# Preparing the next sequence inside the last head pair of a latent-attention stage: two tiles per step, projections spread over steps, score pieces inside the output tiles

## The chip, the cores and the metric

The kernel runs on one NeuronCore of one Trainium2 chip. The metric is the device time of one execution in microseconds (us). The kernel before takes 2420.44 us (median of 3 runs, 2420.27 to 2422.87).

## What is computed

A transformer-like stack on x of shape (2, 1024, 256) in float32: a mixture of experts, attention, the experts again, a LoRA mixture, a latent attention, and the LoRA mixture again. The change touches the latent attention alone. The reference of that part, for two sequences of 1024 tokens and 16 heads (8 pairs of heads):

```python
c_q = _rmsnorm(x @ Wq_down, q_norm_w)                       # 48 wide
q = (c_q @ Wq_up).reshape(b, s, H, HD).transpose(0, 2, 1, 3)
q_rope = _apply_rope((x @ Wq_rope).reshape(b, s, H, RD), cos, sin)
c_kv = _rmsnorm(x @ Wkv_down, kv_norm_w)                    # 64 wide
k = (c_kv @ Wk_up).reshape(b, s, H, HD).transpose(0, 2, 1, 3)
v = (c_kv @ Wv_up).reshape(b, s, H, HD).transpose(0, 2, 1, 3)
k_rope = _apply_rope((x @ Wk_rope).reshape(b, s, H, RD), cos, sin)
scores = (einsum(q, k) + einsum(q_rope, k_rope)) * (HD + RD) ** (-0.5)
out = einsum(softmax(scores), v)
out = out.transpose(0, 2, 1, 3).reshape(b, s, H * HD) @ Wout
```

x enters through a layer norm, and the result is added to x.

## The kernel before, in words

`mla_stage` (from L1475 on) writes one program for each engine by hand and orders them with semaphores; no scheduler stands between. Each sequence b has 8 head pairs. A pair (`pair`) is 16 steps s: the queries come in two blocks of 512 (s < 8 and s >= 8), and in each block the keys in 8 tiles of 128. In a step TensorE computes the scores of one key tile for both heads (`scores_of`, L1752, six matmuls of 512 columns, since each float32 product is made of three reduced ones), ScalarE takes the exponentials into PT (`exp_of`, L1930), TensorE multiplies the latent values with the probabilities of the step before (`values_of`, L1761), and GpSimd adds up the probabilities (`sums`, L1654). At the end of a block TensorE brings the sums across partitions (`denominators`, L1768), and VectorE inverts them (`reciprocals`, L2074, four instructions) and writes the block's latent output LA (`latent_out`, L2079).

Ahead of a pair stand its row maxima. They come from rough scores in pieces (`rough_scores`, L1733, one matmul of 512 columns each), each reduced by VectorE (`maxima`, L2062) into MXP. Of the 32 pieces of a pair, 22 (NLATE) are made before its step 0, in PSUM banks B and C in turn, and 10 in steps 2 to 6 (EARLY), all in bank A. `block_max` (L2068), `max_rows` (L1740, four transposes) and `max_copies` (L1917) turn the maxima into a row of the query operand.

Before its first pair a sequence needs a front: `normalized` (L160: the rows of 128 tokens, in one of two buffers), `xn_transposes` (L1673), `high_rows` (L1875) and `low_rows` (L2014), which split them into a high and a low part; `down_projection` (L1683, six matmuls of 112 columns a tile), `latents` (squares and a copy, L1882 and L1884); then for all tiles `latent_scales` (L2020 to L2028: mean squares, a reciprocal, and 16 instructions that write the normalised latents CN), with `latent_deviations` on ScalarE between them (a square root, with an activation table load before and after it); `latent_transposes` (L1690), `latent_highs` (L1893) and `latent_lows` (L2033); and the first pair's projections (`first_projections`, L1701 and L1708), their rotary products on VectorE (`first_rotary`, L2042 to L2049), the high parts on ScalarE (`highs`, L1905) and the low parts on VectorE (`lows`, L2056). SyncE places the parts in the operand buffers by DMA (`placed`, L1595 and L1599); half 1 of the projections may not be rotated before the DMAs of half 0 have landed, since they read the same buffers, and the next pair's rough scores wait for all of them.

For the second sequence this front is woven into the last pair (pair 7) of the first sequence, in the branches `if after`. Each engine has such branches, at the same steps: one tile of 128 tokens per step in steps 0 to 8, the scales in step 9 (RMS_AT), the latent transposes in steps 10 and 11 (TURN_AT), and half 0 and half 1 of the projections in steps 12 and 13 (FIRST_AT), each half in one go:

```python
RMS_AT, TURN_AT, FIRST_AT = TB + 1, (TB + 2, TB + 3), (TB + 4, TB + 5)
BESIDE = 3
```

After the last pair comes the output projection of the sequence, 8 tiles of `up_projection` (L1781, PSUM banks 4 and 5 in turn) with `updated` on VectorE (L2151, L2153), and beside it the 22 rough pieces of the next pair: two before the first tile, then BESIDE pieces behind each tile.

The functions that the diff touches, and what calls them:

## Time and profile before

| | |
|---|---|
| median of 3 runs | 2420.44 us |
| profiled execution, its own time | 2423.66 us |
| its span, first to last instruction | 2421.9 us |
| PE, DVE, ACT, POOL busy | 83%, 53%, 33%, 33% of the span |
| mean granted TensorE clock | 0.92 of full speed |
| first matmul of the first sequence's pair 7, step 0 | 1712.17 us |
| first matmul of its output projection | 1803.93 us |
| first matmul of the second sequence's pair 0 | 1847.62 us |

PE is TensorE, DVE VectorE, ACT ScalarE, POOL GpSimd, SPq the DMA queue of SyncE. Times in rows are us from the span's start. In a timeline row the first number is the start, the second the duration, and the bracket at the end the idle time of the engine just before and who ended it. The busy share is an average over the whole program; the change lies in the 135 us from 1712 to 1848, so the rows come from there.

### The profile page before, as it was taken

Reading aid. Unit: us, or ns where it says so; the run is one execution under the profiler, and the core shown is the slowest. Engines: PE = TensorE matmul, PEld = TensorE weight load, DVE = VectorE, ACT = ScalarE, POOL = GpSimd, SP = SyncE. Lnnn points to the kernel's source line nnn. Section 1 sums busy time; section 2 is a strip of 40 time slices with the busy share of each in tenths; the row PEclk is TensorE's granted clock in tenths of the full one; section 3 lists DMA queues with packets and bytes.
Section 4 is the critical chain, followed back from the end, with each engine's and each line's share of the span. In section 5 each row is a group of like instructions: output and inputs, shape, how many; then the busy total and the mean of one; then the engine's idle time right before and its main releaser. Section 6 shows DMA issues by size and latency. Waiting matters only on the chain. (4 is left out here: it accounts for less than half of the span.)

```text
span 2421.9 us, 30646 instructions
## 1 busy us (share of the span) xinstructions
PE 2018.4 (83%) x8676; PEld 1249.4 (52%) x8677; DVE 1283.6 (53%) x2888; ACT 790.0 (33%) x1298; POOL 805.5 (33%) x622
## 2 busy tenths in 40 slices
PE   4499947899898569982669999999969999999996
PEld 4266624555454446652545555555546555555465
DVE  3322245677775512224546666666655666666525
ACT  1022232554545112221223333333422333333312
POOL 2200051221212400005004555555522555555631
PEclk9999967899989579995758999999989999999998
DMA  7311133222320821124032222222031222222101
GB/s 311 137 61 61 61 99 38 35 27 28 52 27 1 345 77 60 59 67 149 6 78 48 53 53 52 52 52 52 5 78 30 50 50 52 52 52 52 29 1 46
DMA packets 85575, 159.78 MB, mean 66 GB/s; under 512 B 14881, under 2 KB 49265, under 8 KB 83185
## 3 DMA queue, kind: packets, MB, share of 16 engines
q1 hardware_dynamic: 63216, 127.25, 20.3%
q0 software_dynamic: 6144, 16.79, 2.1%
q10 hardware_dynamic: 16128, 14.69, 1.7%
q8 instruction: 42, 0.69, 0.1%
q14 instruction: 45, 0.36, 0.1%
HBM read 69.34 MB, written 27.39 MB: 40 GB/s over the span
## 5 line engine op out<-in xcount | busy, mean ns | idle before, releaser
L1654 POOL TENSOR_TENSOR mla_PS<-mla_PS,mla_PT 128x1024 f32<-128x1024 f32 x192 | 458.1, 2386 | 240.9 <-ACT mla_PT L1930 238.4
L2062 DVE TENSOR_REDUCE mla_MXP<-PS 128x1 f32<-128x512 f32 x512 | 342.3, 688 | 232.7 <-PE PS L1733 228.2
L1930 ACT ACTIVATE mla_PT<-PS 128x1024 f32<-128x1024 f32 x256 | 262.6, 1026 | 393.7 <-PE PS L1752 393.3
L1761 PE MATMUL PS<-mla_PT,mla_CN 128*64 128x512 f32 x1024 | 276.1, 618 | 0.2
L1733 PE MATMUL PS<-mla_KH,mla_QH 113*128 113x512 f32 x512 | 213.1, 454 | 35.4 <-DVE mla_MXP L2062 17.9
L446 DVE COPY moe_HT<-PS 128x512 f32<-128x512 f32 x96 | 66.4, 691 | 319.3 <-PE PS L556 313.1
L1752 PE MATMUL PS<-mla_QH,mla_KH 113*128 113x512 f32 x512 | 213.1, 416 | 0.3 <-ACT mla_QH L1917 0.3
L1752 PE MATMUL PS<-mla_QL,mla_KH 113*128 113x512 f32 x512 | 203.9, 398 | 0.0
L1752 PE MATMUL PS<-mla_QH,mla_KL 113*128 113x512 f32 x512 | 202.5, 395 | 0.0
L1733 PEld LDWEIGHTS PS<-mla_KH,mla_QH 113*128 113x128 f32 x512 | 90.6, 193 | 199.8 <-DVE mla_MXP L2062 132.7
L1011 ACT ACTIVATE att_PT<-PS 128x1024 f32<-128x1024 f32 (+1 forms) x192 | 152.5, 812 | 94.3 <-PE PS L851 92.6
L550 PE MATMUL PS<-W,moe_ST 128*128 x384 | 176.8, 604 | 2.7 <-DVE moe_ST L441 2.7
L564 PE MATMUL PS<-moe_W,moe_HT 128*128 x768 | 173.7, 379 | 0.0
L830 PE MATMUL PS<-att_KT,att_QT 128*128 128x512 f32 (+3 forms) x384 | 146.6, 427 | 28.4 <-DVE att_MX L1112 10.1
L1654 POOL TENSOR_TENSOR mla_PS<-mla_PT 128x1024 f32<-128x1024 f32 x32 | 76.3, 2383 | 271.2 <-ACT mla_PT L1930 271.2
L1110 DVE CUSTOM_DVE_ANT_0 PS<-PS,att_SEEN 128x128 f32<-128x128 f32 (+3 forms) x256 | 122.8, 508 | 53.9 <-PE PS L830 51.7
L564 PEld LDWEIGHTS PS<-moe_W,moe_HT 128*128 128x128 f32 x768 | 142.2, 190 | 17.3
L2074 DVE RECIPROCAL PS<-PS 128x128 f32<-128x128 f32 x128 | 108.8, 918 | 69.2 <-PE PS L1768 69.2
L1752 PEld LDWEIGHTS PS<-mla_QH,mla_KH 113*128 113x128 f32 x512 | 97.6, 191 | 76.3 <-issue 30.7
L730 POOL TENSOR_SCALAR_AFFINE_SELECT att_PT<-att_PT 128x256 f32<-128x256 f32 x128 | 52.1, 407 | 252.3 <-ACT att_PT L1011 252.3
L830 PEld LDWEIGHTS PS<-att_KT,att_QT 128*128 128x128 f32 x384 | 75.1, 212 | 107.2 <-DVE att_MX L1112 38.5
L851 PE MATMUL PS<-att_QT,att_KT 128*128 128x512 f32 (+3 forms) x384 | 121.5, 402 | 0.0
(274 smaller groups left out, 3102.0 us busy)
## 6 DMA issues: line engine op xcount, KB each, us to landing
W<-in_W_dram SPq DMA_DIRECT2D x8, 2048.0 KB
moe_W<-in_W_dram SPq DMA_DIRECT2D x8, 2048.0 KB
moe_XS<-slots_in SPq DMA_DIRECT2D x100, 128.0 KB, 2.0
slots_out<-moe_YS ACTq DMA_DIRECT2D x96, 128.0 KB, 1.7
mla_QH<-mla_SH SPq DMA_DIRECT2D x64, 128.0 KB, 2.4
mla_KH<-mla_SH SPq DMA_DIRECT2D x64, 128.0 KB, 2.4
mla_QL<-mla_SL SPq DMA_DIRECT2D x64, 128.0 KB, 2.4
mla_KL<-mla_SL SPq DMA_DIRECT2D x64, 128.0 KB, 2.4
```

The costliest lines, as they stand in the source:

```text
L550: ins = pe.matmul(bank(2 + u)[:, :], ST[:, u, k, :], g.W1[:, experts[u], k, :], start=(k == 0), stop=(k == KD - 1))
L564: ins = pe.matmul(bank(6 + u)[:, 0:D], HT[:, u, k, :], W2[:, experts[u], k, :], start=(k == 0), stop=(k == KF - 1))
L830: ins = pe.matmul(out[:, m, :], QT[:, H % 2, h, i * P:(i + 1) * P], KT[:, H % 2, h // 2, k0:k0 + w], start=(m == 0), stop=(m == len(hs) - 1))
L851: ins = pe.matmul(st_banks(s)[:, hh, c0:HB], KT[:, G % 2, pair, j * P:(j + 1) * P], QT[:, G % 2, 2 * pair + hh, q * HB + c0:(q + 1) * HB], ...
L1011: act.activation(PT[:, kk % 2, 2 * pair:2 * pair + 2, c0:HB], st_banks(s)[:, :, c0:HB], ACT.Exp, scale=SEQ ** -0.5).then_inc(s_p.handle, 1)
L1110: ins = dve.tensor_tensor_reduce(part, part, seen, 1.0, LEAST, ALU.mult, ALU.max, MX[:, q, c, h, t:t + 1])
L1654: pool.tensor_tensor(PS[:, :], PT[:, slot(0), :] if k == 1 else PS[:, :], PT[:, slot(k), :], ALU.add).then_inc(s_ps.handle, 1)
L1733: pe.matmul(bank(piece_bank(n))[:, :], QH[USED, buf, h, tile * P:(tile + 1) * P], KH[USED, buf, h, c * HB:(c + 1) * HB], start=True, stop= ...
L1752: ins = pe.matmul(bank(st_bank(s, h))[:, :], kk[USED, buf, h, ks], qq[USED, buf, h, qs], start=(n == 0), stop=(n == 2))
L1761: ins = pe.matmul(bank(6)[h * DKVL:(h + 1) * DKVL, :], CN[:, b, k, 0:DKVL], PT[:, slot(k), h * HB:(h + 1) * HB], start=(k == 0), stop=(k = ...
L1930: act.activation(PT[:, slot(k), :], banks(st_bank(s, 0), 2)[:, :], ACT.Exp, scale=MLA_SCALE).then_inc(s_p.handle, 1)
L2062: dve.tensor_reduce(MXP[:, n // NPC, c, h, t:t + 1], bank(piece_bank(n))[:, :], AX_X, ALU.max).then_inc(s_mx.handle, 1)
```

## The change

The front in pair 7 and the pieces beside the output projection are ordered anew; no arithmetic is added or dropped.

- Two tiles per step: `xn_transposes`, `high_rows`, `low_rows` take tiles 2s and 2s+1 in steps 0 to 3 (FRONT = 4), `down_projection` and `latents` tiles 2s-2 and 2s-1 in steps 1 to 4. On TensorE the down projections move from the end of a step to right behind its scores.
- The mean squares and the square root move to step 5 (SCALE_AT); the 16 instructions that write CN become `latent_rows`, in step 7 (ROWS_AT). Both halves of `latent_transposes`, and the highs and lows of the latents, move to step 8 (TURN_AT).
- The projections move from two lumps in steps 12 and 13 to steps 9, 11, 12, 13 and 15, right behind the scores, with their products, rotations, highs and lows in steps 9 to 15.
- In the output projection each tile takes its pieces behind its third, sixth and eighth product (BESIDE = (2, 5, 7)) and not behind the tile; `maxima` comes ahead of `updated` on VectorE, and `block_max` for the next pair one tile earlier, `max_rows` ahead of the seventh tile.

```diff
-    RMS_AT, TURN_AT, FIRST_AT = TB + 1, (TB + 2, TB + 3), (TB + 4, TB + 5)
-    BESIDE = 3
+    FRONT, SCALE_AT, ROWS_AT, TURN_AT = TB // 2, TB // 2 + 1, TB - 1, TB
+    FIRST_AT = {9: ((0, 0), (0, 1)), 11: ((0, 2),), 12: ((1, 1),), 13: ((1, 0),), 15: ((1, 2),)}
+    BESIDE = (2, 5, 7)
...
+        def beside(i):
+
+            done = [min(2 + len(BESIDE) * n, NLATE) for n in (i, i + 1)]
+            return range(*done)
...
-                    def up_projection(b, i):
+                    def up_projection(b, i, pieces=()):
...
-                        ins.then_inc(s_o.handle, 1)
+                            if k == NP1 - 1:
+                                ins.then_inc(s_o.handle, 1)
+                            if k in BESIDE:
+                                rough_scores((b + 1) * NP1, 0, pieces[BESIDE.index(k):BESIDE.index(k) + 1])
...
                             scores_of(it, buf, s, first and s < 2)
+                            if after:
+                                if 0 < s <= FRONT:
+                                    for j in range(2 * s - 2, 2 * s):
+                                        down_projection(after, j)
+                                if s == TURN_AT:
+                                    for half in range(2):
+                                        latent_transposes(after, half)
+                                if s in FIRST_AT:
+                                    first_projections(after, FIRST_AT[s])
...
-                            if after:
-                                if s < TB:
-                                    xn_transposes(after, s)
-                                if 0 < s <= TB:
-                                    down_projection(after, s - 1)
-                                if s in TURN_AT:
-                                    latent_transposes(after, TURN_AT.index(s))
-                                if s in FIRST_AT:
-                                    first_projections(after, FIRST_AT.index(s))
+                            if after and s < FRONT:
+                                for j in range(2 * s, 2 * s + 2):
+                                    xn_transposes(after, j)
...
-                        up_projection(b, i)
-                        if b + 1 < BATCH:
-                            if i == TB - 2:
-                                max_rows(after, 0)
-                            rough_scores(after, 0, range(min(2 + BESIDE * i, NLATE), min(2 + BESIDE * (i + 1), NLATE)))
+                        if b + 1 < BATCH and i == TB - 2:
+                            max_rows(after, 0)
+                        up_projection(b, i, beside(i) if b + 1 < BATCH else ())
...
+                                if s == TURN_AT:
+                                    for half in range(2):
+                                        latent_highs(after, half)
+                                if s == 10:
+                                    highs(it + 1, 0, (0, 1))
+                                if s == 11:
+                                    highs(it + 1, 0, (2,))
+                                if s == 14:
+                                    highs(it + 1, 1, (0, 1))
+                                if s == 15:
+                                    highs(it + 1, 1, (2,))
...
+                            if after and s == ROWS_AT:
+                                latent_rows(after)
                             maxima(near, todo[:1])
...
+                                if s < FRONT:
+                                    for j in range(2 * s, 2 * s + 2):
+                                        low_rows(after, j)
+                                    for j in range(2 * s + 2, min(2 * s + 4, TB)):
+                                        normalized(after, j)
+                                if s == SCALE_AT:
                                     latent_scales(after)
...
+                                if s == 9:
+                                    products(it + 1, 0, 0)
+                                    products(it + 1, 0, 1)
+                                if s == 10:
+                                    rotated(it + 1, 0)
+                                    lows(it + 1, 0, (0, 1))
+                                if s == 11:
+                                    lows(it + 1, 0, (2,))
+                                if s == 12:
+                                    products(it + 1, 1, 1)
+                                if s == 13:
+                                    products(it + 1, 1, 0)
+                                    rotated(it + 1, 1)
+                                if s == 14:
+                                    lows(it + 1, 1, (0, 1))
+                                if s == 15:
+                                    lows(it + 1, 1, (2,))
...
                     for i in range(TB):
+                        if b + 1 < BATCH:
+                            if i == TB - 3:
+                                block_max(after, 0)
+                            maxima(after, beside(i))
                         updated(b, i)
```

The order on TensorE in steps 8 and 9 of pair 7. Before, step 8 ends in a tile's down projection and step 9 has nothing but scores and values (mla_PT, mla_CN); this is the end of step 8 and step 9:

```order
L1683 MATMUL PS<-mla_WdownL,mla_XTH 128x112
L1752 MATMUL PS<-mla_QH,mla_KH 128x512
L1752 MATMUL PS<-mla_QL,mla_KH 128x512
L1752 MATMUL PS<-mla_QH,mla_KL 128x512
L1761 MATMUL PS<-mla_PT,mla_CN 64x512 x2
L1752 MATMUL PS<-mla_QH,mla_KH 128x512
```

In the change, the end of step 8's scores and the start of step 9 (L1758 scores, L1696 latent transposes, L1774 denominators, L1767 values, L1707 projections):

```order
L1758 MATMUL PS<-mla_QH,mla_KL 128x512
L1696 MATMUL PS<-C,mla_CN 112x128 x8
L1774 MATMUL PS<-mla_PS,C 64x512 x2
L1767 MATMUL PS<-mla_PT,mla_CN 64x512 x2
L1758 MATMUL PS<-mla_QH,mla_KH 128x512
...
L1758 MATMUL PS<-mla_QH,mla_KL 128x512
L1707 MATMUL PS<-mla_XTH,mla_WpairH 128x512
```

The eight latent transposes now stand ahead of the first block's denominators, and the first projections behind the scores of step 9.

VectorE around the same place in the change (L2094 reciprocals of the denominators, L2053 lows of the latents, L2062 first rotary product of the projections; ahead of them the 16 instructions that write mla_CN, of which the last two are shown):

```order
L2047 SCALAR_TENSOR_TENSOR mla_CN<-mla_SH,mla_RS,mla_norms 128x48
L2048 SCALAR_TENSOR_TENSOR mla_CN<-mla_SH,mla_RS,mla_norms 128x64
L2094 RECIPROCAL PS<-PS 128x128 x4
L2053 TENSOR_TENSOR mla_CTL<-PS,mla_CTH 112x512 x2
L2062 TENSOR_TENSOR mla_SL<-PS,mla_rope 128x512
```

Before, the reciprocals (L2074) stood ahead of the 16 instructions, with one tile's low rows and the mean squares between:

```order
L2068 TENSOR_TENSOR mla_MB<-mla_MXP 128x2x4
L2074 RECIPROCAL PS<-PS 128x128 x2
L2014 TENSOR_TENSOR mla_XTL<-PS,mla_XTH 128x2x128
L2074 RECIPROCAL PS<-PS 128x128 x2
L2020 TENSOR_SCALAR mla_SE<-mla_SS 128x8 x2
L2023 RECIPROCAL mla_RS<-mla_SD 128x16
```

So the reciprocals are now behind the writing of CN, and the lows of the latents, for which the first projections wait, behind the reciprocals.

TensorE in the output projection before (L1781 a tile's products, L1733 pieces):

```order
L1781 MATMUL PS<-mla_UV,mla_LA 128x256 x8
L1733 MATMUL PS<-mla_KH,mla_QH 128x512 x3
L1781 MATMUL PS<-mla_UV,mla_LA 128x256 x8
L1733 MATMUL PS<-mla_KH,mla_QH 128x512 x3
```

and in the change (L1787, L1739):

```order
L1787 MATMUL PS<-mla_UV,mla_LA 128x256 x3
L1739 MATMUL PS<-mla_KH,mla_QH 128x512
L1787 MATMUL PS<-mla_UV,mla_LA 128x256 x3
L1739 MATMUL PS<-mla_KH,mla_QH 128x512
L1787 MATMUL PS<-mla_UV,mla_LA 128x256 x2
L1739 MATMUL PS<-mla_KH,mla_QH 128x512
```

No two pieces stand next to each other any more behind the first two.

## Rows read from the trace of the kernel before

**Rows 1.** Windows: busy time by engine, then granted clock, DMA share and GB/s.
```profile
1767.60:1803.90 36.30, 23.99 (x72) 12.30 (x70) 15.76 (x24) 7.90 (x13) 11.20 (x6) 0.81 0.50 114
...
2277.50:2326.90 49.40, 46.19 (x180) 21.94 (x181) 16.23 (x21) 19.23 (x21) 33.35 (x14) 1.00 0.00 1
```
**Rows 2.** Timeline, PE: denominators around both sequences' pair 7, then the output projection's start.
```profile
1714.69 1.08 PE L1768 MATMUL PS<-mla_PS,C 128*64 128x512 f32 x4 [0.96 <-POOL mla_PS L1654]
...
1798.63 1.08 PE L1768 MATMUL PS<-mla_PS,C 128*64 128x512 f32 x4 [1.44 <-POOL mla_PS L1654]
...
1803.93 5.30 PE L1781 MATMUL PS<-mla_UV,mla_LA 128*128 128x256 f32 x16 [3.55 <-DVE mla_LA L2079]
```
**Rows 3.** Waits of PE from 1713 to 1799: total, times, longest.
```profile
PE PS L1708 <- DVE mla_SL L2056: 7.2, 2, 3.7
PE PS L1690 <- DVE mla_CN L2028: 4.1, 2, 2.8
```
**Rows 4.** Timeline, PE: down projection and scores of step 9; values of two steps.
```profile
1750.12 0.32 PE L1683 MATMUL PS<-mla_WdownH,mla_XTH 128*128 128x112 f32 x1 [1.34 <-DVE mla_XTL L2014]
...
1750.84 0.45 PE L1752 MATMUL PS<-mla_QH,mla_KH 113*128 113x512 f32 x1
...
1752.38 1.08 PE L1761 MATMUL PS<-mla_PT,mla_CN 128*64 128x512 f32 x4
...
1754.98 1.08 PE L1761 MATMUL PS<-mla_PT,mla_CN 128*64 128x512 f32 x4
```
**Rows 5.** Timeline, DVE and POOL in steps 0 and 1 of pair 7.
```profile
1715.82 3.40 DVE L2074 RECIPROCAL PS<-PS 128x128 f32<-128x128 f32 x4 [0.71 <-PE PS L1768]
...
1719.51 2.39 POOL L1654 TENSOR_TENSOR mla_PS<-mla_PT 128x1024 f32<-128x1024 f32 x1 [4.87 <-ACT mla_PT L1930]
...
1720.04 2.01 DVE L160 TENSOR_SCALAR mla_SL<-X,MV,RS 128x256 f32<-128x256 f32 x1
```
**Rows 6.** Timeline, ACT, DVE and POOL around the square root and CN, steps 9 to 11.
```profile
1753.53 1.28 ACT L1888 ACT_TABLE_LOAD   x1
...
1756.45 1.02 ACT L1930 ACTIVATE mla_PT<-PS 128x1024 f32<-128x1024 f32 x1
1756.53 0.26 DVE L2027 SCALAR_TENSOR_TENSOR mla_CN<-mla_SH,mla_RS,mla_norms 128x48 f32<-128x48 f32 x1
...
1757.55 2.48 POOL L1654 TENSOR_TENSOR mla_PS<-mla_PS,mla_PT 128x1024 f32<-128x1024 f32 x1 [1.58 <-ACT mla_PT L1930]
1757.65 2.44 DVE L2027 SCALAR_TENSOR_TENSOR mla_CN<-mla_SH,mla_RS,mla_norms 128x48 f32<-128x48 f32 x1
```
**Rows 7.** Windows with a low clock, columns as in rows 1.
```profile
1763.20:1766.30 3.10, 3.06 (x10) 2.56 (x10) 1.88 (x3) 0.59 (x1) 0.00 (x0) 0.52 0.00 0
...
1803.90:1809.30 5.40, 5.37 (x17) 4.44 (x18) 1.21 (x3) 0.00 (x0) 0.00 (x0) 0.70 0.53 86
```
**Rows 8.** Timeline, SPq and DVE: placing DMAs of half 0, then of half 1.
```profile
1773.91 0.60 SPq L1595 DMA_DIRECT2D mla_QH<-mla_SH  x1
...
1782.24 0.69 DVE L2042 TENSOR_TENSOR mla_SL<-PS,mla_rope 128x512 f32<-128x512 f32 x1 [5.08 <-DMA mla_KL<-mla_SL]
...
1786.71 0.60 SPq L1595 DMA_DIRECT2D mla_QH<-mla_SH  x1
...
1793.12 1.23 SPq L1599 DMA_DIRECT2D mla_KL<-mla_SL  x2
```
**Rows 9.** Timeline, PE: output tiles and pieces.
```profile
1811.13 3.62 PE L1781 MATMUL PS<-mla_UV,mla_LA 128*128 128x256 f32 x16
1814.40 0.81 PE L1733 MATMUL PS<-mla_KH,mla_QH 113*128 113x512 f32 x2
1816.31 0.50 PE L1733 MATMUL PS<-mla_KH,mla_QH 113*128 113x512 f32 x1 [1.10 <-DVE mla_MXP L2062]
1816.65 3.62 PE L1781 MATMUL PS<-mla_UV,mla_LA 128*128 128x256 f32 x16
...
1843.39 0.66 PE L1740 MATMUL PS<-C,mla_MB 128*128 128x128 f32 x4 [1.04 <-DVE mla_MB L2068]
```

More of the change, by code:

```diff
@@ L1769, in denominators, with first_projections @@
                         ins.then_inc(s_dn.handle, 1)
-                    def first_projections(b, half):
-                        if half == 0:
+                    def first_projections(b, parts):
+                        if parts[0] == (0, 0):
                             pe.wait_ge(s_ctl.handle, s_ctl.at(2 * (b + 1)))
-                        for what in ((0, 1, 2), (1, 0, 2))[half]:
+                        for half, what in parts:
                             project(b * NP1, half, what)
-                    def up_projection(b, i):
+                    def up_projection(b, i, pieces=()):
                         if i >= 2:
@@ L1842, in _ @@
                             latent_transposes(0, half)
-                        for half in range(2):
-                            first_projections(0, half)
+                        first_projections(0, ((0, 0), (0, 1), (0, 2), (1, 1), (1, 0), (1, 2)))
                         pe.wait_ge(s_fill.handle, s_fill.at(64))
@@ L2161, in _ @@
                         latent_scales(0)
+                        latent_rows(0)
                         for half in range(2):
```

33 lines of the change are left out of this document (11 added, 22 removed).

## Prediction

> **What bounds the kernel now.** I first read the busy shares by stretch. In the last pair of the first sequence, from the lump of projections on, TensorE is busy for 24.0 of 36.3 us at a granted clock of 0.81 [rows 1]. The same pair of the second sequence, which has no front to prepare, takes 49.4 us from its first denominators to its last, with TensorE busy for 46.2 at full clock [rows 1]. With the front it takes 1798.63 - 1714.69 = 83.9 us [rows 2]. So the front costs 34.5 us.
>
> How much of that is work? The projections are 24 matmuls of 512 columns and the latent keys 6 more; a step of six such matmuls and its four value matmuls takes 2.60 us, 1.54 for the six [rows 4], which I read as 0.23 each back to back and a change of operand: 30 x 0.23 = 6.9. A down projection takes 0.72 [rows 4], eight take 5.8. For the 24 transposes I take 2.7, about as much a column. Work W is thus 15.4, and 34.5 - 15.4 = 19.1 us are waits and slow clock. The list of TensorE's waits names 7.2 us for the lows (L2056) inside the two lumps and 4.1 us for CN [rows 3], a down projection adds 1.34 [rows 4]; the remaining 6.5 us are mostly matmuls at half clock.
>
> The second place is the output projection. A tile with three pieces takes 1816.65 - 1811.13 = 5.52 us: 3.27 for its products, then two pieces, a wait of 1.10 for the maximum of the one, and the third piece [rows 9]. With only two banks, the third piece waits for the reduction of the first.
>
> **The front, part by part.** W is moved, not changed, so I count the waits that are left or new, at the step where TensorE meets them.
>
> *Steps 0 to 4, two tiles a step.* VectorE inverts the denominators from 1715.82 to 1719.2 [rows 5] and then takes the low rows of tiles 0 and 1. Before, only the one of tile 0 stood between; now the second comes 0.4 later, at about 1719.9. The down projections now stand right behind scores(1), which with one more pair of transposes ahead of them end at 1718.5. TensorE waits 1.4 us. Then `normalized` for tiles 2 and 3 comes while GpSimd adds: the row for it took 2.01 us at that place, against 0.4 of its own, ending with GpSimd's instruction (1719.51 + 2.39 = 1721.90) [rows 5]; one more of them behind it delays the transposes by some 0.2. From step 2 on VectorE and ScalarE have a whole step for two tiles, 1.6 us of low rows and normalising beside at most three maxima of 0.7, in steps of 4.5 to 5 us: no wait. The wait of 1.34 us for the low rows of tile 7, which the reciprocals of step 7 held up, is gone. I charge 1.6.
>
> *Step 5, the square root.* ScalarE loads a table, takes the root and loads again: its next exponential began at 1756.45, 2.9 us after the first load at 1753.53 [rows 6]. In step 5 it waits for VectorE's mean squares behind the last maximum, so exp(6) ends about 5 us after exp(5). TensorE has scores, two pieces and values for that time: nothing, or up to 1 us.
>
> *Step 7 and 8, CN.* The 16 instructions take 0.19 us each while GpSimd is idle, six from 1756.53 to 1757.65, but one that meets a sum waits for its end: 2.44 us [rows 6]. In step 7 two sums (k = 6 and 7) run one behind the other, 2.4 us each, from the end of exp(6). I take it that both are met, a choice by the row's own two engines taking turns: three instructions ahead of the first, one between, and twelve behind the second, so the first half of CN is there 2.25 us after scores(8) end and the second after 1.0 more with its transposes between. If VectorE kept the sums out, these 3.2 us would be 0; the other bound is one more sum, 2.4 us, as step 8 itself has none. I take 3.2.
>
> *Step 8 and 9, the chain to the first projection.* It is new that the latent transposes stand ahead of the denominators, and the lows of the latents behind all four reciprocals. From the start of the denominators it takes 1.1 us and 3.4 [rows 2, 5] for these and 1.3 for two lows; TensorE has the denominators 0.9, values(7) 1.0 and scores(9) 1.45 against it. It waits 5.8 - 3.3 = 2.5 us, with values(8) queued behind.
>
> *Steps 9 to 15.* Every part of the projections now has between one and two steps (2.6 to 4 us) until its bank is wanted: products and rotations are eight instructions of 0.6 us, spread over four steps. The parts free their banks just in time (the keys of half 0 want the first lows, which I find 0.2 us ahead). The placing DMAs take from 1773.91 to 1782.24, 8.3 us, until half 1 may be rotated [rows 8]; here that holds up VectorE, not TensorE, since half 1's keys are only wanted in step 15. The 7.2 us [rows 3] and the slow clock that they bring go.
>
> Sum for the pair: 49.4 + 15.4 + (1.6 + 3.2 + 2.5) = 72.1 against 83.9, a gain of 11.8.
>
> *The end of the pair.* Before, the output projection began 5.3 us after the denominators [rows 2], through four reciprocals and LA. Ahead of it stand two pieces that want every placing DMA of half 1. These took from 1786.71 to 1793.12 + 1.23, 7.65 us of issuing for twelve, 0.64 each. Of half 0's 8.3 us eight issues are 5.1, so landing took at most 3.2; I take 2.4, since one issue there may have been held up, and come to 10.05 us [rows 8]. The highs of half 1 now come behind exp(14), some 3.9 us ahead of the last denominators, so the pieces start 6.15 us behind these and the output projection 7.1. That is 1.8 us more: a new wait of TensorE for SyncE's DMAs.
>
> **The output projection.** With a piece behind the third, sixth and eighth product the reductions have over 1 us each, and a tile should take 3.27 + 3 x 0.34 = 4.29 us, not 5.52 [rows 9]. Five such tiles give 6.15; the first, with the slow clock, about 1.1; the seventh loses the wait of 1.04 us for the block maximum [rows 9] and part of one reduction, 1.2. In all 8.4. VectorE has 3 x 0.64 + 0.9 = 2.8 us of work in 4.3. Bounds: 6 if each lone piece costs 0.1 us more at each change of operand, 8.9 if none does.
>
> **The clock.** After a wait of 2.8 us [rows 3] the granted clock fell to 0.52, between the level of 1.2 and that of 2.4 GHz, for 3.1 us [rows 7]: a loss of 1.5 us. After waits of 1.34 us it did not. The waits of 2.25 and 2.5 us in steps 8 and 9 are near the first: I charge one such fall, and 0.5 more for the longer wait ahead of the output projection, which already begins at 0.70 [rows 7]. Together 2.0.
>
> The Trainium skill, "TensorE: Matmul & The Clock Gate" (§ Part 4: PE-mode transpose), says that transposes do not raise the clock as other matmuls do. By that rule the eight latent transposes between the two waits would help nothing, and the loss would be that of the rival below; by the row above it is 1.5.
>
> **Sum.** 11.8 - 1.8 + 8.4 - 2.0 = 16.4 us gained. The profiled execution took 2423.66 (span 2421.9), so it would come to 2407.3; the runs' median is 3.2 lower, and 2420.44 - 16.4 = **2404.0 us**. A measurement of this kernel can tell 0.2%, 4.8 us, from no change.
>
> **Rivals.**
> 1. *Slow clock over steps 8 to 12.* The waits of steps 8 and 9 leave about 6 us of work in 12, and the clock could stay at half until the projections are through: 6.4 us at 0.50 is what followed the wait in the second lump, a loss of 3.2 for each such stretch. Two of them cost 6.4, not 1.5: 2409. For: two waits of over 2 us close together. Against: between 1750 and 1763, with two waits of 1.35, the clock held.
> 2. *The waits only move.* If each part of the projections waits some 1.5 us for its high or low part, because ScalarE takes them behind the exponential of the same step, steps 11 to 15 give back 4 x 1.5 = 6 us, and the DMAs of half 1 start later by as much again as TensorE gains: 2410. For: my margins there are 0.2 to 1 us. Against: ScalarE is busy for only 7.9 of 36.3 us there [rows 1].
> 3. *Better.* VectorE finds GpSimd idle for most of CN, and no fall of clock: 3.2 + 1.5 us more, 2399.
> 4. *Slower.* A half clock that holds on. The first output tile took 5.30 us at 0.70 of the clock, a later one 3.62 [rows 2, 7, 9], a factor of 1.46; at half clock I take 1.7. If the waits of step 8 bring it down and it stays down for the 28 us of work in steps 8 to 15, that costs 20 us, and on through three output tiles (3 x 1.65) 5 more: 25 - 16.4 - 1.5 = 7 us slower, 2427. It decides from about 33 us of half clock on. Against: the fall after the longest wait but the lumps lasted 3.1 us [rows 7], and the one in the second lump 6.4.
>
> **How the numbers follow.** The forecast's own case has 0.58 (2400 to 2408), rival 1 0.13, rival 2 0.14, rival 3 0.10, rival 4 0.03; 0.02 is left for the loss of the front's whole gain, 8 us from the output projection alone, partly given back. The range runs from 2397.5, a little beyond rival 3, to 2411.5, beyond rivals 1 and 2. Faster by over 4.8 us: 0.94. Within: 0.03. Slower: 0.03.
>
> **What would show it.** In the new profile pair 7 should take about 72 us between denominators; TensorE's waits for the lows (L2056 before) should be gone but for one of at most 1 us, those for CN some 3 us, and a wait of about 2.5 us ahead of the first projection in step 9. The first output tile should start some 7 us after the denominators, with two rough scores just ahead released by a DMA, and tiles should follow at 4.3 us with no wait of a piece for its maximum. The forecast is wrong if tiles take over 4.8 us, if the clock is under 0.8 over steps 9 to 15, or if the pair takes over 77 us.

## The result, and the profile after

| | before | changed |
|---|---|---|
| median | 2420.7 us (4 runs, 2420.27 to 2422.87) | 2397.67 us (4 runs, 2390.74 to 2399.9) |
| ratio | 1 | 0.9898, 95% interval 0.9877 to 0.9919 |
| profiled execution, its own time | 2423.66 us | 2390.74 us |
| span | 2421.9 us | 2389.0 us |

The changed kernel is faster, by 23.0 us between the medians, or by 24.7 us (19.6 to 29.8) by the ratio. The forecast was a gain of 16.4 us, to 2404.0. That time was too long: by the ratio it is 2395.8 (2420.44 x 0.9898), below the range's lower end of 2397.5; the median of the four runs, 2397.67, lies just at that end.

The profiled execution of the changed kernel is its fastest run, 7 us below its median, and it is already 11.05 us ahead where pair 7 begins: the first denominators stand at 1703.64, and at 1714.69 before [rows 2]. No instruction ahead of that place was changed. So I compare by landmarks inside the latent attention (instructions that both kernels have): the first denominators of pair 7, its last ones, the first matmul of the output projection, and the first scores of the second sequence.

| from the profiles, us | pair 7 | its end to the output projection | output projection | together |
|---|---|---|---|---|
| before | 83.94 | 5.30 | 43.69 | 132.93 |
| forecast, without the clock's 2.0 | 72.1 | 7.1 | 35.3 | 114.5 |
| changed | 71.74 | 6.42 | 33.64 | 111.80 |

That is 21.1 us less than before. What comes behind the last landmark takes 573.6 us against 574.3, so all but 0.7 us of the rest of the 32.9 us between the two spans lies ahead of pair 7.

Windows of the changed kernel, in the columns of [rows 1]: pair 7, its end, and most of the output projection.

```profile
1703.60:1775.40 71.80, 64.64 (x284) 36.48 (x284) 43.94 (x76) 33.08 (x81) 33.27 (x14) 0.95 0.18 40
1775.40:1782.00 6.60, 2.25 (x7) 1.21 (x8) 4.48 (x6) 0.45 (x2) 1.67 (x2) 0.89 0.78 202
1782.00:1817.00 35.00, 35.00 (x159) 30.14 (x158) 21.04 (x39) 1.18 (x2) 0.00 (x0) 0.97 0.09 16
```

TensorE is busy for 64.6 of pair 7's 71.8 us, and in the output projection the whole time.

TensorE's waits in pair 7 of the changed kernel (total, times, longest), answering to [rows 3]:

```profile
PE PS L1696 <- DVE mla_CN L2048: 2.2, 2, 1.8
PE PS L1774 <- POOL mla_PS L1660: 1.8, 2, 1.0
PE PS L1707 <- DVE mla_CTL L2053: 1.4, 1, 1.4
PE PS L1689 <- DVE mla_XTL L2032: 1.0, 1, 1.0
PE PS L1739 <- DVE mla_MXP L2082: 0.8, 1, 0.8
```

The 7.2 us for the lows are gone. In their place stand a wait of 2.2 us for CN in step 8, one of 1.4 us for the latents' lows in step 9, and one of 1.0 us for the low rows in step 1, each at the place that the forecast names.

Timeline of VectorE and GpSimd in step 7, answering to [rows 6]:

```profile
1734.84 4.89 POOL L1660 TENSOR_TENSOR mla_PS<-mla_PS,mla_PT 128x1024 f32<-128x1024 f32 x2 [2.86 <-ACT mla_PT L1939]
1734.92 2.38 DVE L2048 SCALAR_TENSOR_TENSOR mla_CN<-mla_SH,mla_RS,mla_norms 128x64 f32<-128x64 f32 x1
1737.22 0.26 DVE L2047 SCALAR_TENSOR_TENSOR mla_CN<-mla_SH,mla_RS,mla_norms 128x48 f32<-128x48 f32 x1
1737.40 2.41 DVE L2048 SCALAR_TENSOR_TENSOR mla_CN<-mla_SH,mla_RS,mla_norms 128x64 f32<-128x64 f32 x1
```

Two sums back to back each caught one of the 16 instructions; three had run ahead of the first, one ran free between them. The Trainium skill, "SBUF — State Buffer" (§ SBUF: two separate sides), describes such a pattern: a VectorE instruction with two inputs in SBUF and a GpSimd instruction that reads SBUF lock the pair of ports that the two engines share, and who comes first keeps it for a whole instruction. The trace agrees, with 2.38 and 2.41 us for instructions of 0.28 that have two inputs in SBUF (mla_SH and mla_norms).

Timeline of TensorE in steps 8 and 9:

```profile
1740.24 1.10 PE L1696 MATMUL PS<-C,mla_CN 128*112 128x128 f32 x4 [1.77 <-DVE mla_CN L2048]
1741.74 1.10 PE L1696 MATMUL PS<-C,mla_CN 128*112 128x128 f32 x4 [0.40 <-DVE mla_CN L2048]
1742.78 1.98 PE L1774 MATMUL PS<-mla_PS,C 128*64 128x512 f32 x4
1744.54 1.92 PE L1767 MATMUL PS<-mla_PT,mla_CN 128*64 128x512 f32 x4
...
1749.43 0.50 PE L1707 MATMUL PS<-mla_XTH,mla_WpairH 128*128 128x512 f32 x1 [1.39 <-DVE mla_CTL L2053]
```

and the window from the first transpose to the end of the values:

```profile
1739.80:1746.40 6.60, 5.76 (x17) 2.16 (x17) 3.49 (x13) 0.00 (x0) 0.00 (x0) 0.50 0.00 0
```

The clock fell to 0.50 of full, the level of 1.2 GHz, for 6.6 us: denominators and values took 1.98 and 1.92 us where they take 1.08 [rows 2, 4].

What stands between these denominators and the first projection is VectorE's: the reciprocals, which wait for the denominators, and then the lows of the latents.

```profile
1744.80 3.40 DVE L2094 RECIPROCAL PS<-PS 128x128 f32<-128x128 f32 x4 [3.11 <-PE PS L1774]
1748.11 1.27 DVE L2053 TENSOR_TENSOR mla_CTL<-PS,mla_CTH 112x512 fp32r<-112x512 f32 x2
```

The same place in the kernel before, at full clock:

```profile
1746.85 1.08 PE L1768 MATMUL PS<-mla_PS,C 128*64 128x512 f32 x4
1747.98 1.78 DVE L2074 RECIPROCAL PS<-PS 128x128 f32<-128x128 f32 x2 [5.21 <-PE PS L1768]
```

From the start of the denominators to the first reciprocal it takes 1744.80 - 1742.78 = 2.02 us at the slow clock and 1747.98 - 1746.85 = 1.13 at the full one.

The start of the output projection and its second tile:

```profile
1775.38 1.08 PE L1774 MATMUL PS<-mla_PS,C 128*64 128x512 f32 x4 [0.88 <-POOL mla_PS L1660]
1780.81 1.19 PE L1739 MATMUL PS<-mla_KH,mla_QH 113*128 113x512 f32 x2 [4.35 <-DMA mla_KL<-mla_SL]
1781.80 2.52 PE L1787 MATMUL PS<-mla_UV,mla_LA 128*128 128x256 f32 x6
...
1787.02 1.46 PE L1787 MATMUL PS<-mla_UV,mla_LA 128*128 128x256 f32 x6
1788.13 0.58 PE L1739 MATMUL PS<-mla_KH,mla_QH 113*128 113x512 f32 x1
1788.55 1.46 PE L1787 MATMUL PS<-mla_UV,mla_LA 128*128 128x256 f32 x6
1789.66 0.58 PE L1739 MATMUL PS<-mla_KH,mla_QH 113*128 113x512 f32 x1
1790.08 1.03 PE L1787 MATMUL PS<-mla_UV,mla_LA 128*128 128x256 f32 x4
1790.76 0.58 PE L1739 MATMUL PS<-mla_KH,mla_QH 113*128 113x512 f32 x1
1791.18 1.46 PE L1787 MATMUL PS<-mla_UV,mla_LA 128*128 128x256 f32 x6
```

The new wait is there: two pieces released by a DMA, and the output projection 6.42 us behind the denominators, not 5.3. A tile takes 1791.18 - 1787.02 = 4.16 us, with no wait.

### The profile page after: what moved, and what is told of

Read it like the earlier page. It is cut to its first block and busy times, and to the rows that moved or that the text cites. A ratio compares the mean times of both kernels' runs of the same rounds, so it can differ in the third digit from the quotient of the medians.

```text
span 2389.0 us, 30646 instructions
## 1 busy us (share of the span) xinstructions
PE 2009.3 (84%) x8676; PEld 1245.7 (52%) x8677; DVE 1283.1 (54%) x2888; ACT 788.3 (33%) x1298; POOL 806.0 (34%) x622
## 5 line engine op out<-in xcount | busy, mean ns | idle before, releaser
L1767 PE MATMUL PS<-mla_PT,mla_CN 128*64 128x512 f32 x1024 | 275.4, 616 | 0.1
L1739 PE MATMUL PS<-mla_KH,mla_QH 113*128 113x512 f32 x512 | 216.7, 459 | 31.3 <-DMA mla_KL<-mla_SL 20.1
L1758 PE MATMUL PS<-mla_QH,mla_KH 113*128 113x512 f32 x512 | 211.3, 413 | 1.0 <-ACT mla_QH L1926 1.0
L1758 PE MATMUL PS<-mla_QL,mla_KH 113*128 113x512 f32 x512 | 202.6, 396 | 0.0
L1758 PE MATMUL PS<-mla_QH,mla_KL 113*128 113x512 f32 x512 | 201.1, 393 | 0.0
L1739 PEld LDWEIGHTS PS<-mla_KH,mla_QH 113*128 113x128 f32 x512 | 90.8, 193 | 193.5 <-DVE mla_MXP L2082 123.5
L830 PE MATMUL PS<-att_KT,att_QT 128*128 128x512 f32 (+3 forms) x384 | 145.4, 422 | 21.9 <-DVE att_MX L1112 10.0
L2094 DVE RECIPROCAL PS<-PS 128x128 f32<-128x128 f32 x128 | 108.7, 918 | 59.8 <-PE PS L1774 59.8
L1758 PEld LDWEIGHTS PS<-mla_QH,mla_KH 113*128 113x128 f32 x512 | 96.7, 189 | 80.5 <-issue 34.2
```

What stands on the lines that cost most here:

```text
L830: ins = pe.matmul(out[:, m, :], QT[:, H % 2, h, i * P:(i + 1) * P], KT[:, H % 2, h // 2, k0:k0 + w], start=(m == 0), stop=(m == len(hs) - 1))
L1739: pe.matmul(bank(piece_bank(n))[:, :], QH[USED, buf, h, tile * P:(tile + 1) * P], KH[USED, buf, h, c * HB:(c + 1) * HB], start=True, stop= ...
L1758: ins = pe.matmul(bank(st_bank(s, h))[:, :], kk[USED, buf, h, ks], qq[USED, buf, h, qs], start=(n == 0), stop=(n == 2))
L1767: ins = pe.matmul(bank(6)[h * DKVL:(h + 1) * DKVL, :], CN[:, b, k, 0:DKVL], PT[:, slot(k), h * HB:(h + 1) * HB], start=(k == 0), stop=(k = ...
```

## Experiments

For each kernel the landmarks of its profile, since whole times wander by more than most of these effects. The stretch that both kernels share up to pair 7 ends between 1700.9 and 1714.7 us in the fourteen profiles, with no order by edit. Six profiles have the same program in pair 7: the change, the change again, front alone, pieces behind the tile, two pieces and one, first tile first. Five of them take 71.4 to 71.7 us. In two pieces and one it is 72.99, with a slow stretch in step 1 that the others do not have (clock 0.50 from 1717.5 to 1720.5, from the value matmuls of that step on):

```profile
1716.89 1.75 PE L1767 MATMUL PS<-mla_PT,mla_CN 128*64 128x512 f32 x4
1718.58 1.12 PE L1679 MATMUL PS<-C,mla_SL 128*128 128x128 f32 x4
```

In the change these took 1.08 and 0.76 us. The same extra stretch is in the profiles of projections in lumps and of lows first with first tile first. Its cost, 1.0 to 1.3 us, has to be kept apart from what an edit does.

| us | pair 7 | end | output projection | together | ratio to before, 95% interval |
|---|---|---|---|---|---|
| before, again | 84.53 | 5.30 | 44.05 | 133.88 | 1.0003 (0.9993 to 1.0014) |
| changed, again | 71.69 | 6.31 | 34.00 | 112.00 | 0.9904 (0.9888 to 0.9921) |
| front alone | 71.43 | 6.41 | 44.51 | 122.35 | 0.9961 (0.9947 to 0.9975) |
| tiles alone | 84.60 | 5.30 | 34.63 | 124.53 | 0.9969 (0.9955 to 0.9983) |
| projections in lumps | 84.93 | 5.30 | 35.38 | 125.61 | 0.9964 (0.9950 to 0.9978) |
| pieces behind the tile | 71.70 | 6.43 | 38.65 | 116.78 | 0.9935 (0.9912 to 0.9958) |
| two pieces and one | 72.99 | 6.39 | 33.75 | 113.13 | 0.9914 (0.9897 to 0.9931) |
| lows first | 70.41 | 6.32 | 34.69 | 111.42 | 0.9907 (0.9885 to 0.9930) |
| first tile first | 71.70 | 5.39 | 34.88 | 111.97 | 0.9914 (0.9891 to 0.9938) |
| lows first, first tile first | 71.44 | 5.39 | 35.66 | 112.49 | 0.9896 (0.9878 to 0.9914) |
| values first | 72.83 | 6.40 | 34.51 | 113.74 | 0.9924 (0.9901 to 0.9948) |
| values first, lows first | 68.60 | 6.35 | 35.09 | 110.04 | 0.9905 (0.9886 to 0.9925) |

### Both kernels again

No edit.

> The kernel before against itself, to see how far two series of the same program lie apart. Theory 1 (the gain is all in the last pair and the output projection, 21.1 us between landmarks of the two profiles): ratio 1.000 within 0.002, and from the first denominators of pair 7 to the first scores of the second sequence 132.9 us within 0.5, as in the profile of before. Theory 2 (the stages ahead of the latent attention wander by several us from run to run): the series spreads over 5 us or more, and the time to the first denominators of pair 7 (1714.69 us before, 1703.64 in the changed kernel) moves by some us here too.

> The changed kernel once more. Theory 1: the stretch from the first denominators of pair 7 to the second sequence's first scores takes 111.8 us within 0.5, and the median lies 21 to 22 us below before (2399). Theory 3 (the change also makes something faster outside this stretch): the median lies 24 us or more below before, and the missing 3 us are found in the rest of the latent attention.

Before against itself gives 1.0003; the 20 other runs of it in the same series go from 2412.65 to 2427.27 us. So theory 2 holds: the program wanders by several us, and in the two profiles pair 7 begins 3.25 us apart (1714.69 and 1711.44). Of theory 1 only the ratio holds: the stretch is 133.88 us, 0.95 off and not within 0.5. The changed kernel again lies 23.7 us below (2396.37 against 2420.1; by the ratio 19.1 to 27.1), and its stretch is 112.0 us. Against the 132.93 and 133.88 of before that is 21 to 22 us. Theory 3's other 2 us would have to be behind the stretch; there it is 573.9 against 574.5 us, 0.6. The difference lies inside the interval and is not explained further.

### One half of the change at a time

Front alone: the change, with the output projection as before.

```diff
-                        if b + 1 < BATCH and i == TB - 2:
-                            max_rows(after, 0)
-                        up_projection(b, i, beside(i) if b + 1 < BATCH else ())
+                        up_projection(b, i)
+                        if b + 1 < BATCH:
+                            if i == TB - 2:
+                                max_rows(after, 0)
+                            rough_scores(after, 0, beside(i))
```

with `updated` ahead of `block_max` and `maxima` on VectorE, as before. Tiles alone: the kernel before, with the new `up_projection`, `BESIDE` and loops over the tiles.

> The front in pair 7 as in the change, the output projection's tiles and pieces as before. Theory 1 (the parts add): pair 7 takes 71.7 us, the tiles 43.7 (5.52 each), 11 us below before: 2409.5. Rival (the tiles gain only because pieces and clock come differently out of the new pair): the sum of this gain and that of the tiles alone is more than 2 us off 21.

> The output projection's tiles and pieces as in the change, the front as before. Theory 1: pair 7 takes 83.9 us, a tile 4.16 us, the stretch of tiles 33.6 or up to 1 us more for the first tile at the slow clock, 9.5 us below before: 2411. My prediction's price of a tile, 4.29, would give 8.4 us: 2412.

The front alone gains 12.5 to 13.1 us in pair 7 and gives back 1.1 at its end; the tiles alone gain 9.1 to 9.4. Stretch against stretch of before (132.93) the two gains are 10.6 and 8.4, together 19.0, against 21.1 of the change and 20.9 of its second profile. They add within 2.1 us, at the limit of what the rival asks for, while the two profiles of before lie 0.95 us apart themselves (against the second of them the two gains are 11.5 and 9.35, together 20.9, against 21.9 to 22.1). So the rival is not excluded for an effect of 1 to 2 us. In tiles alone the output projection takes 34.6 us and not 33.6 to 34.0; behind the old end of the pair its first tile takes 6.21 us, against 5.22 in the change, with more of the slow clock.

### The projections in two lumps again

```diff
-    FIRST_AT = {9: ((0, 0), (0, 1)), 11: ((0, 2),), 12: ((1, 1),), 13: ((1, 0),), 15: ((1, 2),)}
+    FIRST_AT = {12: ((0, 0), (0, 1), (0, 2)), 13: ((1, 1), (1, 0), (1, 2))}
```

with `highs` of a half on ScalarE and `first_rotary` on VectorE in the same step.

> The change, but the first pair's projections in two lumps, half 0 in step 12 and half 1 in step 13, with their rotary products, highs and lows, as before (TensorE's lumps stand behind the scores here). Theory 1 (the gain of the pair comes from spreading the projections; two tiles per step only make room for it): the two waits for the lows are back, 3.5 us each, with the slow clock behind them, and pair 7 takes 82 to 85 us, as before the change. Theory 4 (two tiles per step and the front's early end gain by themselves): pair 7 takes 77 us or less.

Pair 7 takes 84.93 us: the whole gain of the pair is gone, although the rows of the next sequence are two tiles a step and CN is written two steps earlier. Two of TensorE's waits:

```profile
PE PS L1714 <- DVE mla_SL L2070: 8.0, 2, 4.5
PE PS L1787 <- DVE mla_LA L2093: 3.6, 1, 3.6
```

The waits for the lows are back, 8.0 us (7.2 before [rows 3]); the second one, 3.6 us for LA, lies behind the pair. Theory 1 holds, theory 4 falls: the early front does not bring the gain by itself; it brings the projections forward to step 9, so that they can be spread. The waits for CN and for the low rows are shorter here than before, by 1.9 and 0.3 us. The slow stretch in step 1 takes back 1 us or more, and the lumps, which stand behind the scores here and behind the values before, wait 0.8 us longer. That the early front is worth nothing at all is therefore not shown.

### Pieces behind the tile, with VectorE's new order

```diff
-                        up_projection(b, i, beside(i) if b + 1 < BATCH else ())
+                        up_projection(b, i)
+                        if b + 1 < BATCH:
+                            rough_scores(after, 0, beside(i))
```

> The change, but all three pieces of a tile behind the tile again; VectorE keeps the new order, maxima ahead of updated. Theory 1 (spreading the pieces gains 1.36 us a tile): 5.52 us a tile. Theory 5 (a part of it is VectorE's order: before, the update of 0.85 us stood ahead of the maximum that the third piece waits for): 4.7 us a tile, and spreading gives only the other 0.5 us.

```profile
1785.20 3.62 PE L1787 MATMUL PS<-mla_UV,mla_LA 128*128 128x256 f32 x16
1788.47 0.83 PE L1739 MATMUL PS<-mla_KH,mla_QH 113*128 113x512 f32 x2
1789.84 0.49 PE L1739 MATMUL PS<-mla_KH,mla_QH 113*128 113x512 f32 x1 [0.55 <-DVE mla_MXP L2084]
1790.18 3.62 PE L1787 MATMUL PS<-mla_UV,mla_LA 128*128 128x256 f32 x16
```

A tile takes 4.98 us, the wait is 0.55 and not 1.10 [rows 9]. So 0.54 of the 1.36 us that a tile gained come from VectorE's order, in which the update no longer stands ahead of the maximum that the third piece waits for; the other 0.82 come from the spreading. Theory 5 has the cause right and its size too large: it expected a tile of 4.7 us. My prediction gave all of it to the spreading.

### Two pieces side by side

The change, with pieces one and two behind a tile's third product and the third piece behind its seventh.

```diff
-    BESIDE = (2, 5, 7)
+    BESIDE, PLACES = (2, 5, 7), {2: slice(0, 2), 6: slice(2, 3)}
...
-                            if k in BESIDE:
-                                rough_scores((b + 1) * NP1, 0, pieces[BESIDE.index(k):BESIDE.index(k) + 1])
+                            if k in PLACES:
+                                rough_scores((b + 1) * NP1, 0, pieces[PLACES[k]])
```

> The change, but each output tile takes two pieces side by side behind its third product and the third piece behind its seventh. No piece should wait for a maximum. Theory 6 (a lone piece among the products is cheap, since TensorE's products there are held up by their weight loads, and each change from products to pieces and back hides some of one: 20 products without pieces take 4.13 us, 0.207 each, so that the pieces of a 4.16 us tile cost 0.29 each, against 0.34 and more in a block of three): with two blocks instead of three a tile takes 4.20 to 4.30 us. Rival (only the waits for the maxima count): 4.16 us.

```profile
1796.33 0.82 PE L1739 MATMUL PS<-mla_KH,mla_QH 113*128 113x512 f32 x2
1796.99 1.89 PE L1787 MATMUL PS<-mla_UV,mla_LA 128*128 128x256 f32 x8
1798.53 0.59 PE L1739 MATMUL PS<-mla_KH,mla_QH 113*128 113x512 f32 x1
1798.95 1.89 PE L1787 MATMUL PS<-mla_UV,mla_LA 128*128 128x256 f32 x8
1800.49 0.82 PE L1739 MATMUL PS<-mla_KH,mla_QH 113*128 113x512 f32 x2
```

A tile takes 1800.49 - 1796.33 = 4.16 us, to the hundredth what three lone pieces take. Theory 6 falls: two blocks of pieces cost the same as three, so the number of changes of operand makes no difference here, and what is left to count are the waits.

### The lows of the latents first

On VectorE in step 8 `latent_lows` ahead of all four reciprocals; on ScalarE `latent_highs` ahead of `out_copy`.

```diff
+                            if after and s == TURN_AT:
+                                for half in range(2):
+                                    latent_lows(after, half)
+                                reciprocals(2 * it, range(4))
-                            if s == 7:
+                            if s == 7 and not after:
                                 reciprocals(2 * it, (2, 3))
-                            if s == 8:
+                            if s == 8 and not after:
                                 reciprocals(2 * it, (0, 1))
```

> The change with the lows of the latents ahead of the reciprocals on VectorE in step 8, and the latent highs ahead of the copy of the values on ScalarE. Theory 1 (the chain reciprocals, then lows, holds the first projections): the wait of 1.4 us in step 9 is gone, pair 7 takes 70.3 us. Rival (the reciprocals, 1.3 us later, hold something else, or the clock's slow stretch sets the time): 71.7 or more.

The wait is gone from the list, the first projection begins 44.6 us behind the first denominators (45.8 in the change), and pair 7 takes 70.41 us, 1.3 less than the change. The moved reciprocals cost nothing that can be seen. The chain was what the forecast said. In the kernel with both edits, below, pair 7 took 71.44: it has the extra slow stretch in step 1.

### The first output tile ahead of the first pieces

```diff
-                        rough_scores(after, 0, range(2))
                     pe.wait_ge(s_la.handle, s_la.at(2 * after))
                     for i in range(TB):
-                        if b + 1 < BATCH and i == TB - 2:
+                        if b + 1 < BATCH and i == TB - 1:
                             max_rows(after, 0)
-                        up_projection(b, i, beside(i) if b + 1 < BATCH else ())
+                        up_projection(b, i, beside(i - 1) if b + 1 < BATCH and i else ())
+                        if b + 1 < BATCH and i == 0:
+                            rough_scores(after, 0, range(2))
```

with the matching order of `maxima` and `block_max` on VectorE.

> The change, but the first two pieces come behind the first output tile, which has none inside, the others one tile later, and the row maxima ahead of the last tile. Theory 1 (the output projection waits for SyncE's placing DMAs through these two pieces): it starts 5.3 us behind the denominators, not 6.4; the two pieces, 0.7 us, then lie in the stretch of the tiles, so that the whole gains 0.4 to 0.9 us. Rival (LA is what it waits for anyway): no change of the 6.4.

> The lows of the latents ahead of the reciprocals, and the first two pieces behind the first output tile, together. If the two gains add: pair 7 takes 69.9 us or less, the output projection begins 5.4 us behind the denominators, and from the first denominators of pair 7 to the second sequence's first scores it is 110.4 us or less, 1.5 us below the change. The time should be 22 to 24 us below before, 1.5 below the change, too little to be told apart by the median.

```profile
1780.83 1.08 PE L1774 MATMUL PS<-mla_PS,C 128*64 128x512 f32 x4 [0.88 <-POOL mla_PS L1660]
1786.22 5.38 PE L1787 MATMUL PS<-mla_UV,mla_LA 128*128 128x256 f32 x16 [4.31 <-DVE mla_LA L2100]
```

The output projection begins 5.39 us behind the denominators, released by LA: the DMAs were what it waited for. But the stretch of the tiles is 0.9 to 1.2 us longer, 0.7 of it the two pieces, the rest mostly the first tile at the slow clock (5.38 us here). Nothing is won in the whole: 111.97 us against 111.80 and 112.00. With the lows first it came to 112.49 where 110.4 was expected. About 1.0 us of that is the extra slow stretch in step 1, and the first tile took 6.17 us; whether the two edits add without these is open.

### Values ahead of the transposes

```diff
                                 if s == TURN_AT:
+                                    values_of(NS * it + s - 1, 2 * it, s - 1)
                                     for half in range(2):
                                         latent_transposes(after, half)
...
-                            if s or not first:
+                            if (s or not first) and not (after and s == TURN_AT):
```

once in the change and once with the lows first.

> The change, but in step 8 TensorE multiplies the values of step 7 ahead of the latent transposes, not behind the denominators. The 1.0 us of values fill a part of the wait of 1.8 us for CN. Theory 7 (that wait is what brings the clock down to half for the 6 us from the transposes on): the wait is 0.8 us, the clock stays at full through step 8, and pair 7 takes 70 us or less. Rival (the fall has another cause, or two waits of 0.8 and 0.4 us beside the one ahead of scores(8) are enough): the clock falls at the same place; since the denominators then end with the same work behind them, pair 7 takes 70.7 us (only the values are saved) or, where the chain over the reciprocals and the lows sets the first projection, up to 71.7.

> The same with the lows of the latents ahead of the reciprocals too, so that nothing but TensorE's own work stands between the transposes and the first projections. Theory 7: no slow stretch in step 8, and pair 7 takes 67 to 68 us. Rival (the clock falls all the same): 69 us. In both cases the values' 1.0 us come off the 69.9 to 70.9 us of the two kernels with the lows ahead.

In the first of the two the wait for CN shrank to 0.78 us and the transposes ran at full clock, but the clock fell just behind them:

```profile
1748.10 0.65 PE L1696 MATMUL PS<-C,mla_CN 128*112 128x128 f32 x4 [0.78 <-DVE mla_CN L2049]
1749.60 0.65 PE L1696 MATMUL PS<-C,mla_CN 128*112 128x128 f32 x4 [0.85 <-DVE mla_CN L2049]
1750.18 1.96 PE L1774 MATMUL PS<-mla_PS,C 128*64 128x512 f32 x4
...
1756.81 0.60 PE L1707 MATMUL PS<-mla_XTH,mla_WpairH 128*128 128x512 f32 x1 [2.37 <-DVE mla_CTL L2054]
```

So the clock also falls behind two waits of 0.8 us around four transposes, with one of 0.7 ahead of them, and theory 7 is wrong that the wait of 1.8 us is needed. And since the values no longer fill the wait for the latents' lows, that wait grew from 1.4 to 2.4 us. The first projection still came 0.45 us earlier against the first denominators (45.34 us behind them, 45.79 in the change), but a second slow stretch covered it, and pair 7 took 72.83. With the lows first the same edit gives 68.60, the shortest pair of all, and the shortest stretch, 110.04 us against 111.8 and 112.0 of the change. One slow stretch was left there, 3.4 us long, so the theory's full clock was not reached. In the whole time (ratio 0.9905, the change again 0.9904) that cannot be told apart; it beats the change in its stretch alone.

## Why the prediction was right and wrong

**Right: where TensorE waits.** The waits of pair 7 are where the forecast put them: 1.6 us charged for steps 0 to 4, measured 1.0 and 0.15; 3.2 for CN, measured 1.77 and 0.40; 2.5 for the latents' lows, measured 1.39. The square root in step 5 cost nothing, as said. CN meets both sums, with three instructions ahead of the first and one between, as I took it. The lump experiment shows that the gain of the pair hangs on the spread projections.

**Right: the new wait.** The DMAs of half 1 took 9.6 us from their first issue (1771.19) to the pieces, 10.05 forecast, and began 4.2 us ahead of the denominators, 3.9 forecast. The output projection began 6.42 us behind them, not 7.1.

**Wrong in size: the output projection.** This is the largest single error. The steps are "a tile should take 3.27 + 3 x 0.34 = 4.29 us" and "the first, with the slow clock, about 1.1": 8.4 us forecast, 10.05 measured. The five middle tiles gained 6.8 (27.60 to 20.79), not 6.15, since a piece between products costs 0.29 us: 16 products at the pace of products without pieces (20 in 4.13 us, from 1811.31 to the first scores at 1815.44) are 3.30 of the 4.16. 0.34 was the spacing of a piece that follows a wait. The first tile, 7.20 us before, takes 5.22, a gain of 1.98: behind the two pieces it has less of the slow stretch in it. In tiles alone, without the new front, it took 6.21, a gain of 0.99, so the forecast's 1.1 fits the old end of the pair and not the new one. The end, 1.26, was right (1.2). And the reason was only half right: two fifths of a tile's gain, 0.54 of 1.36 us, came from VectorE's order.

**Wrong in size: the waits of the pair.** With the fall of the clock charged the pair was put at 73.6 us; it took 71.74. In front alone, where the transposes of the latents ran at full clock or nearly so, the waits for CN were 1.76 and 0.85, together 2.6 and not the 3.2 of "I take 3.2": behind the second sum ten instructions were left and not twelve, since I had not counted the two that were caught. In the change the second of these waits is only 0.40, since the slow transposes fill the rest. Steps 0 to 4 cost 1.15 and not 1.6.

**About right: the price of the fall in the pair.** The fall came, and it was longer than charged, 6.6 us at 0.50 and not 3.1 at 0.52. TensorE's work in it took about 2.6 us longer. By the rows about 1.3 of these came through to the first projection (an estimate), where "I charge one such fall" put 1.5. VectorE's chain begins with the denominators, and these were late and slow: from the second transposes to them it took 1.04 us (1741.74 to 1742.78), 0.58 in values first at full clock, and from them to the reciprocals 2.02, 1.13 before. That is 0.46 + 0.89. The rest did not count: the first transposes' 0.45 lay in the wait for CN, and the values' 0.85 in the wait for the latents' lows, which by the same estimate would have been 2.2 us at full clock, not 1.39. One comparison bears on it: in front alone the clock was down for 3.4 us and not 6.6, from just ahead of the denominators on, and from the second transposes to these it took 0.71 us. The pair was 0.3 us shorter, by just what the denominators came earlier. A pair without any fall was not measured.

**Wrong: the clock ahead of the output projection.** "0.5 more for the longer wait" was charged and did not come. The end of the pair and the first tile came out shorter than forecast, by 0.7 and 0.9 us.

**The account.** 16.4 forecast and 21.1 measured between landmarks. Of the 4.7 us more, 1.9 are from the pair with its clock (0.6 CN, 0.45 steps 0 to 4, 0.3 the wait for the lows and 0.2 the fall, by the estimate above; 0.3 are not split), 1.2 from its end (0.7 the wait for the DMAs, 0.5 the clock), 1.65 from the tiles. The other 2 to 3.6 us up to the medians' 23.0 and the ratio's 24.7 lie in what wanders ahead of pair 7 and within the interval; they are not explained, and it was not tried to hold that part still. The range's lower end had room for no fall of clock and for CN without sums, but not for an output projection above its bound of 8.9 us, nor for the measurement's own width of 5 us to each side.

**The rivals.** The slow clock over steps 8 to 12 (rival 1) came about for half its length: one stretch of 6.6 us in step 8, not two. It cost about 1.3 us by the estimate above and not 3.2, since a part of it lay beside waits. That the waits only move (rival 2) did not happen in steps 11 to 15: the list has none there. A change that makes it happen is the values moved forward alone: the wait for CN lost 1.0 us (1.77 to 0.78), and the one for the lows grew by as much (1.39 to 2.37). The better case (rival 3) did not come either: both sums were met and the clock fell. The time came near its 2399 for other reasons, the output projection and the end of the pair; that is luck for this rival. Of rival 4's long half clock nothing was seen.

## What to carry to other kernels

Time the parts of a wait's chain before moving work into or out of it: moving TensorE's work ahead of a wait for VectorE brought little (the first projection came 0.45 us earlier) until VectorE's chain was shortened too (pair 7 took 72.8 us with the values first, 68.6 with the lows first as well). Price a slow clock by what it delays: charge in full the work that the next wait's chain begins with, and not the work that only fills that wait (here about 1.3 of 2.6 us). And where a lump of dependent steps makes one engine wait for two others by turns, spread it over the iterations of an independent loop: here that made 12 to 13 us of an 85 us pair, while making its inputs ready earlier did not shorten the pair by itself.

## What was not expected of the hardware

- TensorE's clock fell to half behind waits of only 0.78 and 0.85 us around short transposes, after a wait of 0.7, where two waits of 1.34 and 1.35 us, 7 us apart, in the kernel before had left it at 0.99. What stood around the waits was different, and the waits' lengths alone do not tell. The Trainium skill, "TensorE: Matmul & The Clock Gate" (§ Part 4: PE-mode transpose), says that the full clock does not engage for transposes in its transpose mode. Here the four transposes still ran at full clock (0.65 us, 1.10 at the slow one) and the fall came behind them; no run varied the transposes alone, so the rule is neither shown nor refuted.
- A VectorE instruction with its inputs in SBUF that met a GpSimd sum took 2.4 us and not 0.26, and between two sums with nothing between them exactly two such instructions began: one ran free (0.26), the next was caught by the second sum (2.41).
- A wait of 1.10 us in the list was worth more than 1.10: the tile lost 1.36 us with it, of which 0.26 appear in no wait (4.98 - 0.55 = 4.43 with the short wait, 4.16 with none).
- Profiles with the same program in pair 7 differ in where TensorE's clock is low. Two pieces and one had a slow stretch of some 3.4 us in step 1, behind a wait of 1.00 us, where the change had the same wait at the same place and kept its clock.
